# Graph network kernel: where layer 1's transposed counts stand behind the last chunk

## The reference

```python
agg_sum = segment_sum(h[nbr], tgt, n)        # sums over the edges of a node
deg     = segment_sum(ones(E), tgt, n)
agg     = agg_sum / maximum(deg, 1.0)[:, None]
out     = relu(h @ Wl + bl + agg @ Wr + br)
x       = x + out / (norm(out, axis=1) + 1e-6)
```

## Time and profile before

| | us |
|---|---|
| median of 3 runs | 2910.49 |
| lowest and highest run | 2902.32, 2915.22 |
| the profiled execution, its time | 2950.78 |
| the profiled execution, its span | 2949.0 |
| last chunk's copy L882 on ACT, start | 672.38 |
| end of layer 1's sums (L1001 on DVE, 737.45 and 0.46 long) | 737.91 |

### The profile page before, as it was taken

How to read it: one execution, slowest core, us unless ns; L and a number is a source line. 1 busy time by engine, 2 the same in 40 slices (tenths; PEclk the granted TensorE clock), 3 DMA queues, 4 the chain that set the end, 5 groups by cost and what they waited for, 6 DMA issues and landing times.

```text
span 2949.0 us, 51575 instructions
## 1 busy us (share of the span) xinstructions
PE 2371.0 (80%) x12348; PEld 2007.6 (68%) x12453; DVE 1499.2 (51%) x6364; ACT 1215.3 (41%) x5336; POOL 1195.0 (41%) x1243
## 2 busy tenths in 40 slices
PE   2567676766518888888976889999998999999998
PEld 1444444542407787777853778788877888888887
DVE  4567666765515455455533555555564433333333
ACT  2556565653312233333321343434445444444443
POOL 3656566640056666666324665656642100000000
PEclk9977677776755555555568876757679999999999
DMA  3132313233333333333232333323336200000001
GB/s 84 51 103 54 104 52 106 56 94 86 87 96 83 91 92 92 92 92 91 69 85 76 89 90 87 94 76 91 92 87 251 74 26 22 23 23 23 23 23 55
DMA packets 177575, 227.46 MB, mean 77 GB/s; under 512 B 63568, under 2 KB 137625, under 8 KB 177145
## 3 DMA queue, kind: packets, MB, share of 16 engines
q0 software_dynamic: 50176, 131.74, 16.6%
q1 hardware_dynamic: 120286, 88.93, 10.0%
q10 hardware_dynamic: 6810, 3.40, 0.4%
HBM read 183.63 MB, written 40.29 MB: 76 GB/s over the span
## 4 chain that ended last, share of the span: by engine, by line
PE 59%; issue 13%; DVE 11%; another core or an unknown queue 7%; ACT 5%; ACTq 2%; SPq 1%; DMA 1%; POOL 1%; DVEq 0%; POOLq 0%
PE banks L2801 8%; PE banks L2797 8%; PE banks L1706 5%; PE banks L1767 4%; PE banks L1764 4%; PE banks L1765 4%; PE banks L850 3%; PE banks L1770 3%; PE banks L2803 2%; PE banks L2408 2%; PE banks L825 2%; PE banks L1768 2%; PE banks L828 2%; PE banks L841 1%
## 5 line engine op out<-in xcount | busy, mean ns | idle before, releaser
L231 POOL DMA_INDIRECT arena<-value_table,arena x392 | 395.3, 1008 | 387.6 <-DMA ed_table<-arena 169.3
L231 POOL DMA_INDIRECT arena<-gat_table,arena x392 | 394.3, 1006 | 360.4 <-PE banks L1770 184.1
L2797 PE MATMUL banks<-counts,u_parts 128*128 128x448 f32 x1323 | 491.9, 372 | 3.1 <-DVE u_parts L2930 3.1
L2801 PE MATMUL banks<-counts_even,u_parts 128*128 128x448 f32 x1323 | 487.1, 368 | 0.0
L231 POOL DMA_INDIRECT arena<-h_table,arena x392 | 375.4, 958 | 239.1 <-PE banks L828 128.7
L825 PE MATMUL banks<-arena 128*128 128x425 bf16 x392 | 184.8, 471 | 201.5 <-ACT arena L882 104.9
L2981 DVE CAST counts_even<-counts 128x448 fp32r<-128x448 bf16 x450 | 162.9, 390 | 303.9 <-PE banks L2801 275.4
L2797 PEld LDWEIGHTS banks<-counts,u_parts 128*128 128x128 f32 x1323 | 249.7, 189 | 23.9 <-ACT arena L2425 3.3
L1764 PE MATMUL banks<-arena 128*128 128x17 f32 x784 | 227.7, 371 | 46.0 <-issue 26.4
L2801 PEld LDWEIGHTS banks<-counts_even,u_parts 128*128 128x128 f32 x1323 | 249.8, 189 | 21.2 <-ACT counts_even L2905 0.3
L1764 PEld LDWEIGHTS banks<-arena 128*128 128x128 f32 x784 | 201.9, 319 | 54.4 <-issue 28.3
(11 more groups left out here) (286 smaller groups left out, 4883.5 us busy)
## 6 DMA issues: line engine op xcount, KB each, us to landing
adj_rows<-arena SPq DMA_DIRECT2D x4, 4000.0 KB
arena<-ed_table SPq DMA_DIRECT2D x784, 0.5 KB
arena<-turned_rows SPq DMA_DIRECT2D x27, 448.0 KB, 3.3
counts<-adj_rows SPq DMA_DIRECT2D x1, 7200.0 KB, 20.7
arena<-h_table,arena POOLq DMA_INDIRECT x392
arena<-value_table,arena POOLq DMA_INDIRECT x392
arena<-gat_table,arena POOLq DMA_INDIRECT x392
counts<-adj_rows SPq DMA_DIRECT2D x1, 5600.0 KB, 18.1
```

The costliest lines, as they stand in the source:

```text
L231: return e.indirect_dma_start(into, None, table, bass.IndirectOffsetOnAxis(ap=index.bitcast(U32), axis=0))
L2797: e.matmul(banks[:, 2 * r, 0:HALFW], weight, C_odd[:, w0:w0 + HALFW], start=start, stop=stop)
L2801: x = e.matmul(banks[:, 2 * r + 1, 0:HALFW], weight, tile(n), start=start, stop=stop)
```

## The change

From the first unit whose slot is 396 or more (unit 150 of 175, called LATE), turns go to bank 3 and bank 7 in turn, and copies go to four CT buffers in turn, two of them new. Unit 150 waits in addition for the last chunk (l0_acc at NC), since bank 3 and the place of the new buffers belong to the chunks until then. From unit 150 a turn waits for the copy of unit i - 2, and a copy for the sum of unit i - 4. The area early_at moves up by 512 words behind the new buffers.

```diff
-        early_at = L0_at
+        late_at = L0_at
+        early_at = late_at + 2 * QUAD * P // 2
...
+        LATE = next(u.i for u in UNITS if u.slot >= NC + 4)
...
+            CT += [at(late_at + k * QUAD * P // 2, [QUAD * P], BF16) for k in range(2)]
+            counts_of = lambda u: CT[u.i % 2] if u.i < LATE else CT[(2, 3, LATE % 2, (LATE + 1) % 2)[(u.i - LATE) % 4]]
+            turned_of = lambda u: banks[:, 7 if u.i < LATE or (u.i - LATE) % 2 else 3, :].bitcast(BF16)
...
                             e.wait_ge(l0_acc, block_end(u.b))
+                            if u.i == LATE:
+                                e.wait_ge(l0_acc, NC)
                             if u.i:
-                                e.wait_ge(l1_evicted, u.i)
+                                e.wait_ge(l1_evicted, u.i if u.i < LATE else u.i - 1)
                             for s in range(n):
-                                x = e.transpose(banks[:, 7, :].bitcast(BF16)[:, s * P:(s + 1) * P], C[:, s0 + s, u.b * P:(u.b + 1) * P], identb)
+                                x = e.transpose(turned_of(u)[:, s * P:(s + 1) * P], C[:, s0 + s, u.b * P:(u.b + 1) * P], identb)
...
-                            x = e.matmul(banks[:, 5 + u.total % 2, 0:n * P], part_of(u.b, j), CT[u.i % 2][:, 0:n * P],
+                            x = e.matmul(banks[:, 5 + u.total % 2, 0:n * P], part_of(u.b, j), counts_of(u)[:, 0:n * P],
...
                         if u.i >= 2:
-                            e.wait_ge(l1_product, u.i - 1)
-                        e.activation(CT[u.i % 2][:, 0:n * P], banks[:, 7, :].bitcast(BF16)[:, 0:n * P], ACT.Copy, scale=LARGE,
+                            e.wait_ge(l1_product, u.i - 1 if u.i < LATE else u.i - 3)
+                        e.activation(counts_of(u)[:, 0:n * P], turned_of(u)[:, 0:n * P], ACT.Copy, scale=LARGE,
                                      accum_out=indeg_in[:, u.q, u.b:u.b + 1]).then_inc(l1_evicted, 1)
```

## The result

The changed kernel took 2901.93 us in the median of 20 runs (2877.07 to 2924.62). The kernel before, run beside it, took 2927.99 in the median of 20 (2902.32 to 2953.53), its first three runs being those shown ahead of the prediction. The medians are 26.1 us apart. The ratio, which is taken over the runs within 1.5% of their kernel's fastest, is 0.9916, with a 95% interval from 0.9894 to 0.9937: 24.6 us (0.84%) less, beyond the 0.5% that was set as the bound. The forecast was 25.2 us less, and 2885 us.

What follows compares the result with a forecast made beforehand. Turn, sum and copy were taken to run one after another, with PE, ACT and DVE waiting in turn. Ending at 712.7 against 737.91 saves 25.2 us: 2910.49 - 25.2 = 2885 us, forecast range 2875 to 2894, whole range 2873 to 2903.

Steps and rivals of the forecast that it cites:

- The chain: Last stretch of layer work: turn, sum and copy never overlap; removing both waits from unit 150 saves 25.2 us.
- the tail: From the addition of unit 147's total to the closing reduction's end, 61.5 us before; forecast 25.2 us shorter.
- First part: From 676.41 to the first loops behind block 24's split: DVE bounds at the higher clock, 14.1 us saved.
- Second part: From the first loops to the end of the closing reduction: 33.12 us before, 22.0 us forecast.
- the clock behind the pause: After PE stands still from about L + 3 to L + 8 (L: first loops), it starts on the lower clock.
- rival of a lower clock throughout: PE stays at the lower clock from 676.41 to the closing reduction: 17.1 us saved, 2893 us; chance 0.14.
- Carrying on: Next function: waiting for the block diagonal hides nothing; its loads and first products move along with the sums' end.
- the sum: Whole kernel: 25.2 us taken one to one from the median of 2910.49, giving 2885 us.
- The slower rival: Second attention pass starts 25 us earlier against its clock; 2.5 us per 0.01, 2940 us at 0.50; chance 0.06.

Runs made afterwards that it cites:

- the third profile: The kernel before, unedited, profiled a third time: 2923.28 us profiled, 2924.74 us in the median of 8 runs.
- both repeats: The changed kernel, unedited, profiled a second and a third time: 2898.46 and 2902.64 us profiled.

## Why the prediction was right in the change and wrong in the time

**The chain.** Right: the round turn, sum, copy was serial, and undoing both links made the tail 27.8 us shorter in the mean of three profiles each (60.4 against 32.6); 25.2 was forecast. Undoing either link alone gives most of it. That the time agrees so well with 25.2 is in part luck. Two errors cancel: the changed tail was forecast at 36.3 us and takes 32.4 to 32.9, and the tail before was taken as 61.5 from one profile, while the third profile, whose time is the one near the median, has 55.9. Against that one the tail is 23.3 us shorter.

**First part.** 14.3 us was forecast, 12.59 of DVE's work and 1.7 of handing over; 14.11 was measured, and 13.07 in both repeats. The forecast had the clock at 1.00 up to the loops; the repeats show that, while the first profile began at 0.50, so its nearness to 14.3 is chance. DVE alone was named as the bound, and PE was put at 10 us for its units; in the repeats DVE is busy for 11.74 us and PE for 11.91, so they share the bound.

**Second part.** Mis-sized: 22.0 us forecast, 18.8 to 19.5 measured. The term was the clock behind the pause: I let PE run at the lower level for most of it, and it was back on the higher one 11.9 us behind the first loop (698.46 - 686.58). The forecast's own bound for the higher clock was 19.0.

**The clock in the tail.** The rival of a lower clock throughout fails: 0.99 in the dense stretch. The Trainium skill's "A second HAM failure mode: psum-queue depth-cycling" in "TensorE: Matmul & The Clock Gate" ties a swinging clock to work that cycles through PSUM banks, by way of short pieces in which PE is idle. In this trace turns alternate between banks 3 and 7, PE is busy for 8.89 of 9.40 us and the clock is 0.99, so the cycling alone does not bring it about. The clock fell in the pause, in which PE stood still for 5.5 us.

**Carrying on.** Right: no wait for the store of the block diagonal shows behind the tail, and the stretch from the tail's end to the first gather is 88.0 to 90.2 us, against 86.8 to 89.2 before. The remark of the Trainium skill, same title, section "HAM oscillation — how this bites in real kernels", that double-buffering PSUM gave its kernel no further gain does not carry over to this one: a second bank alone took the tail from 60.4 to 33.6 us.

**The step that failed** is the sum: "2910.49 - 25.2 = 2885 for the median", with "the median of a few runs adds 4 or so". The base was the median of three runs; with 17 more it became 2927.99, and sets of 27 and 25 runs have medians of 2925.67 and 2928.74. The three shown lay 17.5 us low, in place of the 4 or so. A sign was there to read: the profiled execution was 40 us longer, and I carried the saving to the median without asking which of the two stood for the kernel. Against the base of the runs beside the changed kernel, 2928 - 25.2 gives 2902.8, and 2901.93 was measured. Why the three lay so low stays open: of the other 77 runs of this kernel 10 are no longer than 2915.22, the longest of the three, so three such runs in a row are unlikely as plain draws, and nothing was run to find what differed.

**The slower rival.** Its mechanism is a good part of the spread, at nearly double the price. The first two profiles of the kernel before are 27.5 and 31.8 us longer than the third; 12.5 and 22.2 of that lie in the second pass, 5.6 and 8.0 in the tail. From 0.76 to 0.69 the second pass grows from 647 to 680 us, 4.6 us for 0.01 of its mean clock, where I had read 2.5 from two windows of one trace. It isn't seen to favour one kernel: the pass takes 658 to 680 us in the three profiles of the kernel before and 647 to 679 in the seven with the change or a part of it. I also used it the wrong way round: from three runs within 12.9 us I concluded that the mean moves by 0.05 at most; ten profiles show 0.07, which by the right price is 32 us. What sets that pass's clock in one execution stays open.

## What to carry to other kernels

Where steps of several engines wait for each other in turn and no engine is full, count the links that close the round. Here breaking one of the two gave most of the gain, and the bank gave more than the buffers. What bounds the stretch next can be sought in the busy times of its engines, which a window gives at once: here DVE and PE were both nearly full in the first part, and DVE behind it. Add a forecast change to a ratio or to a base of many runs, not to the median of three, and read a profiled time far from the runs as a warning that neither may stand for the kernel. A saving read from one profile carries that profile's clock with it: the same tail took 55.9 to 63.9 us in three.

## What the runs showed of the hardware

The granted clock of PE differs from execution to execution in one and the same stretch of a program: 0.69 to 0.73 over the second attention pass in three profiles of the kernel before, 0.69 to 0.76 in all ten, and in the tail of the kernel before 0.70 or 0.87 over the first part (28.38 and 25.43 us). In the changed kernel's first profile it fell from 1.00 to 0.50 while PE stood still for 5.5 us, and was 0.99 again from 698.46 on, 3.6 us after PE had resumed work. Twenty-four additions of 128 by 128 in bf16 on POOL took 8.70 us, 0.36 us each, and DVE's additions of 128 by 512 beside them took 0.69 us, as without them.
